# Squares of the keys on VectorE instead of ScalarE, and 8 wide selector matmuls instead of 64 narrow ones, in an attention and expert layer on 8 cores

## The reference

```python
B, L, DIM, H, DH, NF = 8, 2048, 1024, 16, 64, 64          # attention part
q, k, v = split_heads(x @ Wq.T + bq), split_heads(x @ Wk.T + bk), split_heads(x @ Wv.T + bv)
logits = einsum('bhld,hdf->bhlf', k, W0) - 0.5 * sum(k * k, axis=-1, keepdims=True)
alpha = softmax over all (l, f) of logits, per head
N = einsum('bhlf,bhld->bhfd', alpha, v);  D = sum(alpha, axis=2)
phi = softmax(einsum('bhld,hdf->bhlf', q, W0), axis=-1)
out = einsum('bhlf,bhfd->bhld', phi, N) / (einsum('bhlf,bhf->bhl', phi, D) + 1e-6)
x = layernorm(x + ctx @ Wo.T + bo)
# feed-forward part: one of E = 8 experts per sequence
losses = ... (m1, m2: mean of x and of x*x over the tokens);  idx = argmin(losses, axis=0)
h = relu(x @ down_W[idx] + down_b[idx])                   # D -> R = 64
a = h @ up_W[idx] + up_b[idx]
y = a @ conv_W[idx].T + conv_b[idx]
x = layernorm(x + x @ base_W.T + base_b + y)
```

## Time and profile before

| | |
|---|---|
| median of 2 runs | 609.79 us (609.12 to 610.46) |
| profiled execution, its own time | 613.68 us |
| its span, slowest core (core 6) | 611.9 us |
| spans of the cores | 595.2 to 611.9 us |
| busy on core 6: TensorE, VectorE, ScalarE | 461.6, 243.3, 242.8 us |
| phase 4 on core 6, first key matmul to ME(1) | 235.85 to 287.40 us |

### The profile page before, as it was taken

The page is one execution under the profiler, slowest core; times in us unless marked ns, Lnnn a source line. Parts: engine busy times, 40 slices in busy tenths (PEclk is TensorE's granted clock), DMA queues, the critical chain, the costliest instruction groups (busy, mean ns, idle before and its releaser), DMA issues.

```text
span 611.9 us, 8705 instructions; the slowest of 8 cores (595.2 to 611.9 us)
## 1 busy us (share of the span) xinstructions
PE 461.6 (75%) x2816; PEld 230.6 (38%) x2855; DVE 243.3 (40%) x613; ACT 242.8 (40%) x760; POOL 26.7 (4%) x54
## 2 busy tenths in 40 slices
PE   0579999997877876767666649576597468889984
PEld 0234444443444445656332324243243234333331
DVE  3000024435656652212205143462647771455553
ACT  0133320003565567565606344372546302233233
POOL 2020000000000000000201001011000000000000
PEclk9999999999999997898679787795899978999998
DMA  7749643007000004363799593784909100122222
GB/s 97 117 87 160 119 67 70 1 1 137 2 2 1 2 1 73 76 102 55 130 157 153 87 161 63 130 131 77 166 16 195 31 1 1 55 84 103 104 103 103
DMA packets 10428, 49.26 MB, mean 81 GB/s; under 512 B 1917, under 2 KB 3072, under 8 KB 7889
## 3 DMA queue, kind: packets, MB, share of 16 engines
q0 software_dynamic: 6864, 38.12, 37.7%
q1 hardware_dynamic: 3522, 10.60, 4.7%
HBM read 77.38 MB, written 9.45 MB: 142 GB/s over the span
## 4 chain that ended last, share of the span: by engine, by line
PE 47%; DMA 23%; ACT 12%; DVE 10%; issue 6%; POOL 1%; DVEq 0%; ACTq 0%; POOLq 0%
DMA scr<-wuaug 17%; PE pb L320 8%; PE pb L459 6%; PE pb L279 6%; PE pb L1032 5%; DMA axA<-xT 4%; PE pb L354 4%; ACT scr L390 3%; ACT scr L395 2%; PE pb L582 2%; DMA wg<-wk 2%; PE pb L552 1%; PE pb L413 1%; PE pb L715 1%; PE pb L317 1%
## 5 line engine op out<-in xcount | busy, mean ns | idle before, releaser
L390 ACT ACTIVATE scr<-pb,mxb 128x64 bf16<-128x64 f32 x128 | 42.1, 329 | 94.8 <-DVE mxb L385 94.8
L279 PE MATMUL pb<-axA,wg 128*128 128x512 bf16 x220 | 55.6, 391 | 25.1 <-DMA axA<-xT 24.2
L459 PE MATMUL pb<-wg,scr 128*65 128x512 bf16 x112 | 39.1, 507 | 45.0 <-DMA scr<-wuaug 38.1
L715 PE MATMUL pb<-wg,axD 128*128 128x512 bf16 x243 | 59.8, 387 | 8.4 <-DVE iostg L732 3.3
L1032 PE MATMUL pb<-wg,axC 128*128 128x512 bf16 x234 | 55.4, 378 | 8.2 <-ACT iostg L1074 7.9
L320 PE MATMUL pb<-wg,axA 128*128 128x512 bf16 x220 | 53.4, 379 | 0.3
L354 PE MATMUL pb<-axA,wg 128*128 128x512 bf16 x215 | 52.3, 379 | 1.4 <-DVE axC L327 1.1
L668 ACT ACTIVATE axD<-pb,ddbuf 128x64 bf16<-128x64 f32 x128 | 46.5, 382 | 16.8 <-DVE ddbuf L657 16.4
L674 ACT ACTIVATE axD<-pb,ddbuf 128x64 bf16<-128x64 f32 x128 | 47.1, 389 | 0.0
L284 ACT ACTIVATE axD<-pb,smallsb 128x512 bf16<-128x512 f32 x32 | 22.0, 687 | 59.5 <-PE pb L276 58.5
L395 ACT ACTIVATE scr<-pb,mxb 128x64 bf16<-128x64 f32 x128 | 42.7, 334 | 0.0
(11 more groups left out here) (169 smaller groups left out, 740.1 us busy)
## 6 DMA issues: line engine op xcount, KB each, us to landing
wg<-wct POOLq DMA_DIRECT2D x8, 2048.0 KB, 16.9
out<-iostg SPq DMA_DIRECT2D x16, 512.0 KB, 2.6
axA<-xT POOLq DMA_DIRECT2D x4, 1024.0 KB, 13.7
wg<-wk POOLq DMA_DIRECT2D x2, 1024.0 KB, 10.6
wg<-wv POOLq DMA_DIRECT2D x1, 2048.0 KB, 28.2
wg<-wq POOLq DMA_DIRECT2D x1, 2048.0 KB, 14.8
wg<-wo POOLq DMA_DIRECT2D x1, 2048.0 KB, 15.8
xstg<-xtok POOLq DMA_DIRECT2D x8, 256.0 KB, 11.6
```

The lines of the kernel that those rows point to most:

```text
L279: st=(kc == 0): t.matmul(o, a, b, start=st, stop=False))
L390: sc.activation(o, i_, AF.Exp, bias=b, scale=1.0))
L459: st=(kc == 0): t.matmul(o, a, b, start=st, stop=False))
L715: st=(kc == 0): t.matmul(o, a, b, start=st, stop=False))
```

## The change

The squares of phase 4 are computed by VectorE as a product of the piece with itself, and the key groups wait for VectorE's mark instead of ScalarE's. The call stays at its place in the code. A wait of VectorE for the key groups of the pass before stood ahead of it already. The selection of the down weights is done with one matmul of 512 columns for each expert, and the host lays the down weights out by expert first and chunk second.

```diff
@@ phase 4
             for lb in range(4):
                 src2 = axD[:, c * 2048 + lb * 512: c * 2048 + lb * 512 + 512]
                 dstk = scr[:, SCR_K2 + lb * 512: SCR_K2 + lb * 512 + 512]
-                k2lb[(c, lb)] = emi("scalar", lambda sc, o=dstk, a=src2:
-                                    sc.activation(o, a, AF.Square, bias=0.0,
-                                                  scale=1.0), "sc")
+                k2lb[(c, lb)] = emi("vector", lambda v, o=dstk, a=src2:
+                                    v.tensor_mul(o, a, a), "ve")
             if c >= 1:
                 p4_dcol(c - 1)
...
-                wait("tensor", "sc", k2lb[(c, lb)])
+                wait("tensor", "ve", k2lb[(c, lb)])
@@ selected down weights
-        for c in range(C):
-            for e in range(E):
-                dwe = axD[:, AXD_DW + c * 512 + e * 64:AXD_DW + c * 512 + e * 64 + 64]
-                emi("tensor", lambda t, o=pb[3][:, c * 64:c * 64 + 64],
-                    a=mid128[:, e * 128:e * 128 + 128], b=dwe,
-                    st=(e == 0), sp=(e == E - 1):
-                    t.matmul(o, a, b, start=st, stop=sp),
-                    "pe" if (c == C - 1 and e == E - 1) else None)
+        for e in range(E):
+            dwe = axD[:, AXD_DW + e * 512:AXD_DW + e * 512 + 512]
+            emi("tensor", lambda t, o=pb[3][:, 0:512],
+                a=mid128[:, e * 128:e * 128 + 128], b=dwe,
+                st=(e == 0), sp=(e == E - 1):
+                t.matmul(o, a, b, start=st, stop=sp),
+                "pe" if e == E - 1 else None)
@@ host
-        downW.reshape(8, 8, 128, 64).transpose(2, 1, 0, 3).reshape(128, 4096))
+        downW.reshape(8, 8, 128, 64).transpose(2, 0, 1, 3).reshape(128, 4096))
```

## The result

| | before | changed |
|---|---|---|
| median | 610.75 us (10 runs) | 623.17 us (11 runs) |
| ratio to before | | 1.0214 (1.0175 to 1.0253) |
| profiled execution, its own time | 613.68 us | 620.14 us |
| its spans, mean of the 8 cores | 603.5 us | 612.7 us |

The ratio is taken from the executions in which no die ran at a lowered clock, so it isn't quite that of the two medians. The change makes the kernel 2.1% slower, 13 us (10.7 to 15.5) of 610.75; whether that is over or under 2% the interval leaves open. The spans of the two profiled executions give +9.2 us in the mean of the cores; the time goes by the slowest core, which isn't the same one in every execution.

A forecast was written before the change was run, and what follows sets the result against it. The prediction took a chain of waits as the bound, in phase 4 TensorE waiting for VectorE's ndb writes and dcol copy. Terms 7.5 + 0.4 - 2.0 + 2.0 + 0 = +7.9 us on 609.79 gave about 617.5 us, range 611 to 625.

The forecast's parts named there:

- the terms alone: Whole kernel: the summed terms at their bounds, without the rivals, +3.4 to about +12 us, 613 to 622 us.
- the two slow rivals: Phase 4: low clock in all seven passes, 624.5 us, chance 0.12; products at the 692 ns rate, 624 us, chance 0.07.
- the clock goes in every pass: Phase 4: all seven passes slow, clock term +9 instead of +2, sum +14.9, 624.5 us; chance 0.12.
- the prediction's own signs: Profile after: squares about 0.42 us, long passes near 7.1 us; wrong if phase 4's clock is much lower or steady.
- The squares' length: VectorE in phase 4: a square takes 420 ns, four take 1.5 us, bounds 1.3 and 2.8 us.
- The 692 ns rival: VectorE's squares run at the rate of the add with fp32 PSUM operand: 6.5 us more, 624 us; chance 0.07.
- The place in the queue: Passes 2, 3, 5, 6, 7: squares stand between ndb writes and dcol copy; 5 x 1.5 = 7.5 us lost.
- Pass 4: After ME(0): the first exp no longer waits behind four squares on ScalarE; 2.0 us gained.
- Passes 0 and 1: Start of phase 4: one square added in pass 0, 0.4 us lost; nothing in pass 1.
- The clock: TensorE in phase 4: 1.3 more passes' worth of lower clock at 1.5 us each, 2 us lost; bounds -1.5 to +9.
- the squares are covered: Phase 4: waits for ndb and dcol have slack for the squares; only pass 4's gain remains, -2, 607.8 us; chance 0.08.
- ScalarE was the bound: Phase 4: freed of squares, seven passes go at 4.0 us instead of 5.6; -11, 599 us; chance 0.02.

The follow-up runs named there:

- the added products: Kernel before, squares left on ScalarE, plus four unread products per pass on VectorE where the change puts its squares; ratio 1.0302, phase 4 53.5 us.
- the doubled ones: Changed kernel with each phase 4 product done a second time into an unread buffer, eight ahead of dcol instead of four; ratio 1.0354, phase 4 58.2 us.
- the early squares: Changed kernel with the next pass's squares emitted behind the reciprocal and ahead of the ndb writes; ratio to before 0.9968, phase 4 37.4 us.
- The dummy matmuls: Changed kernel plus unread 512-column matmuls in TensorE's waits of passes 2, 3, 5, 6, 7; ratio to before 1.0037, phase 4 44.2 us.
- the kernel before kept busy: Kernel before plus three unread 512-column matmuls ahead of the pair sum in passes 2, 3, 5, 6, 7; ratio 0.9985, phase 4 39.8 us.
- dcol first and the squares left on ScalarE: Kernel before with only the copy of dcol moved ahead of the ndb writes; ratio 0.9877, phase 4 34.4 us.
- the kernel with early squares and dcol first: Changed kernel with squares emitted ahead of the ndb writes and the dcol copy also moved ahead of them; ratio to before 0.9860, phase 4 33.2 us.
- the kernel with dummy matmuls: Squares and dcol copy ahead of the ndb writes, plus unread 512-column matmuls, two before the third key group, one before the fourth; ratio to before 0.9873, phase 4 34.2 us.

## Why the prediction was right or wrong

Right: the sign, the place and the mechanism of the first edit's larger part, that the second is worth nothing, and that later stages pass the loss on. The time, 623.2, lies in the range of 611 to 625, but 5.7 us over the 617.5 forecast, and over the 613 to 622 of the terms alone. That the range holds it is owed to the two slow rivals, whose 624.5 and 624 it takes in; the time lies nearer to "the clock goes in every pass" than to the forecast. Of the prediction's own signs, the long passes took 8.0 to 8.6 us in the mean, not 7.1, and the granted clock was much lower than before (0.54 to 0.79 in all five long passes of core 4, where the earlier trace rows have two low stretches), which it had named as a sign of being wrong.

*The squares' length.* Forecast 0.42 us, four in 1.5; measured 420 ns and 1.43. The 692 ns rival is out. The estimate of 424 ns by the Trainium skill, VectorE: DVE Perf Modes (The perf-mode tier table), agrees with the trace's 420.

*The place in the queue.* Forecast 7.5 us in five passes; a pass at full clock went from 5.53 to 6.99, 7.3 us. Shown by the added products, by the doubled ones and by the early squares.

*Pass 4.* Forecast -2.0; measured -1.9 from ME(0) to the broadcast.

*Passes 0 and 1.* Forecast +0.4 in pass 0 from one more square, nothing in pass 1. From the end of the last copy of axB to the first key matmul are 0.36 us on every core before and 0.48 after, so the first product adds 0.1 there. The reading that ScalarE's squares "are on the path in one place: pass 4" was wrong. Before, on six of the eight cores, three of them stand in the chain ahead of the first key matmul. They also stand in the chain ahead of the first exp of pass 1, on core 6:

```profile
239.76 0.60 ACT scr L567
240.36 2.08 ACT scr L533 x4
```

On all eight cores that exp starts as the fourth square ends, 6.49 us after the first key matmul in the mean; after the change it is 6.18. From the first key matmul to the first broadcast are 9.8 us in the mean before and 9.6 after (8.8 to 10.0 on single cores). So these two passes are no loss at all, for a forecast one of 0.4.

*The clock: this is the step that was mis-sized.* I took "1.3 more passes' worth: 2 us". The dummy matmuls measured 6.6 us in the changed kernel. Before had 1.8 of its own (40.5 against the 38.7 of the core that kept full clock throughout, in the kernel before kept busy), so the change added 4.9. The terms then add up: 7.3 - 1.9 + 4.9 = 10.3, and 50.8 - 40.5 is 10.3. As the 4.9 is itself a difference of such phase lengths, what this checks is the other two terms: 44.2 - 38.7 is 5.5, and 7.3 - 1.9 is 5.4. The rival "the clock goes in every pass" was right in how often (39 of 40 long passes) and too high in the total, 9 us: it counted seven passes with 1.5 us each, where five have 1.3 (8.33 in the mean, less 6.99). The prediction's sums for it are slightly off as well: 609.79 + 14.9 is 624.7, and with the pass that before already pays taken off, +12.2 is passed at five to six slow passes and not at four. The reading that failed was of the earlier trace rows: from one stretch that had lost the clock and others that had kept it I took it that most passes with 1.5 us more of waiting would keep it. All but one lost it for a part of their length or all of it. The Trainium skill, TensorE: Matmul & The Clock Gate (A second HAM failure mode: psum-queue depth-cycling), on short idles between groups of matmuls that make the clock swing, agrees with the trace here more than I allowed: the granted clock of the passes shown was 0.54 to 0.79, between the two levels, and filling the idles brought it to 1.00 on every core.

*The rest.* 13 us by the runs (10.7 to 15.5) against 10.3 in phase 4. The spans of all cores narrow it down: in the mean of the 8 cores they are 614.4 us over ten executions of the changed kernel and 602.3 to 603.1 over 34 of the kernel before in its three sets, 11.3 to 12.1 us apart. The profiled execution of the changed kernel was below its mean and that of before above its own, which is why they give 9.2. So 1 to 2 us more than the 10.3 are in all cores, and about as much is the slowest core's own. In which stage they are is open: from ME(1) to the end the mean of the cores varies between 314.8 and 322.9 us from one profiled kernel to another.

The rivals "the squares are covered" and "ScalarE was the bound" are refuted for this order of the queues. With the squares early they are covered; with dcol first and the squares left on ScalarE, ScalarE is the bound.

## What to carry to other kernels

An engine that is idle three quarters of the time isn't free: before work is moved to it, look at what stands behind the insertion point in its queue and who waits for that. The same four products cost 7.3 us in one place and nothing in another, four instructions ahead, because there the engine waited for something that was not yet due. And price an added wait of TensorE twice, once for its length and once for the clock of the matmuls behind it: here it was 4.9 us beside 7.3. Dummy matmuls in the wait are a quick way to measure the second part, and here even a way to get it back.

## What the runs showed of the hardware beyond that

Once dcol no longer held TensorE back, another stop appeared that no semaphore explains. Core 3 of the kernel with early squares and dcol first, in pass 6:

```profile
269.08 0.61 ACT scr L568
269.69 1.73 issue
271.42 0.26 PE pb L553
```

The exp that the third key group waits for ended at 269.69; the group came 1.73 us later, where 0.24 is usual. In the kernel with dummy matmuls it is in pass 6 on six of eight cores and makes it 7.3 to 9.2 us long. It falls into the load of ME(1)'s 2 MB of weights; the stretch from 268.60 to 273.00 on core 3 has:

```profile
268.60:273.00 4.40, 1.97 (x23) 1.89 (x21) 0.50 (x3) 1.48 (x3) 0.00 (x0) 0.79 1.02 169
```

a DMA share of 1.02. Dummy matmuls add instructions and it got worse with them, which would fit TensorE waiting for its own instructions behind that load. The records of the DMA queues fit this too. The page counts 24 packets of a queue that it calls instruction (q8), of 16 KB each; on core 3 one of them runs from 269.14 to 270.46, and TensorE goes on 0.96 us after its end. With the dummy matmuls, TensorE's stop in pass 6 ends 1.30 to 1.40 us after the end of such a packet on each of the six cores; on cores 3 and 4 it falls between two matmuls of one key group, where the program has no wait. But such packets also come where nothing stops. No run changed the instructions or the load alone, so the cause stays open. In the kernel before, pass 6 takes 5.53 or 5.54 us on all cores, and in the changed one 8.3 to 8.6.
